# Cross-attention block with MLP on one core: two stages with fp32r operands, against one pipeline over the batches with operands as two fp16 parts

## The reference, cut to what matters

```python
# B=16 batches, L=256 queries, T=256 tokens, D=512, H=16 heads of 32, MLP width 2048, all fp32
q = ln(x, q_norm_g, q_norm_b);  kv = ln(ctx, kv_norm_g, kv_norm_b)
qp = q @ Wq.T + bq;  kp = kv @ Wk.T + bk;  vp = kv @ Wv.T + bv
scores = qh @ kh.T / sqrt(32)                       # per batch and head, 256 x 256
scores += -spatial_scale[h] * dist(query_xy, token_xy) + spatial_offset[h]
scores = where(mask, scores, -inf)
attn = softmax(scores) @ vh                         # per head
x = x + attn @ out_proj_w.T + out_proj_b
h = ln(x, mlp_norm_g, mlp_norm_b)
x = x + gelu(h @ w1.T + b1) @ w2.T + b2             # w1: 2048 x 512, w2: 512 x 2048
```

## Time and profile before

| | us |
|---|---|
| median of 3 runs | 1420.79 (1420.65 to 1423.2) |
| the profiled execution | 1420.8, its span 1419.0, mean clock 0.992 |
| busy: PE, DVE, ACT, POOL | 1381.1, 859.4, 811.9, 706.7 |
| DMA | 120.01 MB, mean 85 GB/s |

### The profile page before, as it was taken

The page is one execution under the profiler, slowest core; times in us unless marked ns, Lnnn a source line. Parts: engine busy times, 40 slices in busy tenths (PEclk is TensorE's granted clock), DMA queues, the critical chain, the costliest instruction groups (busy, mean ns, idle before and its releaser), DMA issues.

```text
span 1419.0 us, 25885 instructions
## 1 busy us (share of the span) xinstructions
PE 1381.1 (97%) x8860; PEld 1166.1 (82%) x8860; DVE 859.4 (61%) x2557; ACT 811.9 (57%) x2003; POOL 706.7 (50%) x1049
## 2 busy tenths in 40 slices
PE   6899999999999999999899999999999999999999
PEld 2589888898888889888688888888888888888887
DVE  6599999999999999989835322232222322223211
ACT  4599989898989999998734323222222222222221
POOL 2588888889888888899621201212012120121200
PEclk9899999999999999999999999999999999999999
DMA  4545555565555556455421100101001010010000
GB/s 172 135 101 126 137 147 144 141 156 134 147 131 130 141 138 157 126 145 147 160 104 38 60 1 0 60 1 60 1 1 60 1 60 1 0 60 0 31 1 30
DMA packets 67076, 120.01 MB, mean 85 GB/s; under 512 B 9088, under 2 KB 9344, under 8 KB 66944
## 3 DMA queue, kind: packets, MB, share of 16 engines
q1 hardware_dynamic: 66944, 118.35, 30.3%
HBM read 50.94 MB, written 16.78 MB: 48 GB/s over the span
## 4 chain that ended last, share of the span: by engine, by line
PE 62%; DVE 16%; POOL 7%; issue 6%; ACT 5%; DMA 2%; SPq 1%; DVEq 0%; ACTq 0%; POOLq 0%
PE ps_s L571 12%; PE ps_qk L557 12%; PE ps_pt L571 12%; PE ps_tr L557 12%; DVE pT L839 4%; PE ps_qk L490 4%; DVE soft L829 3%; POOL soft L1121 3%; POOL soft L1129 2%; PE ps_pt L453 2%; PE ps_vo L516 2%; PE ps_vo L513 2%; DVE qk_parts L845 1%; ACT soft L657 1%; DVE stats L877 1%
## 5 line engine op out<-in xcount | busy, mean ns | idle before, releaser
L978 DVE TENSOR_TENSOR hid<-gelu,hid 128x512 fp32r<-128x512 f32 x128 | 94.7, 740 | 509.7 <-ACT hid L747 509.7
L1121 POOL TENSOR_SCALAR soft<-soft,row_stats 128x256 f32<-128x256 f32 x512 | 246.6, 495 | 58.8 <-DVE row_stats L835 58.2
L657 ACT ACTIVATE soft<-soft,row_stats 128x256 f32<-128x256 f32 x512 | 255.5, 507 | 0.3
L490 PE MATMUL ps_qk<-xT,w_qkv_sb 128*128 128x256 f32 x1536 | 230.8, 293 | 3.3 <-DVE qk_parts L845 3.2
L490 PEld LDWEIGHTS ps_qk<-xT,w_qkv_sb 128*128 128x128 f32 x1536 | 196.9, 192 | 4.3 <-DVE qk_parts L845 4.1
L571 PE MATMUL ps_s<-w,hid 128*128 128x512 f32 x768 | 199.2, 395 | 0.0
L1129 POOL TENSOR_SCALAR soft<-dist,scale_neg,offset 128x512 f32<-128x512 f32 x256 | 197.1, 770 | 0.2 <-ACT dist L681 0.2
L571 PE MATMUL ps_pt<-w,hid 128*128 128x512 f32 x768 | 195.3, 390 | 0.0
L829 DVE CUSTOM_DVE_ANT_0 soft<-ps_s,soft 128x256 f32<-128x256 f32 x512 | 193.0, 413 | 3.8 <-POOL soft L1129 2.0
L557 PE MATMUL ps_qk<-hT,w 128*128 128x512 f32 x768 | 184.8, 389 | 0.9 <-ACT gelu L744 0.9
L557 PE MATMUL ps_tr<-hT,w 128*128 128x512 f32 x768 | 184.6, 389 | 0.0
(11 more groups left out here) (97 smaller groups left out, 2012.7 us busy)
## 6 DMA issues: line engine op xcount, KB each, us to landing
stack<-qk_parts SPq DMA_DIRECT2D x256, 192.0 KB
raw<-in_ctx SPq DMA_DIRECT2D x32, 256.0 KB, 3.2
raw<-in_x SPq DMA_DIRECT2D x32, 256.0 KB, 3.1
x_t<-in_x SPq DMA_DIRECT2D x32, 256.0 KB, 2.6
x_scratch<-x_t SPq DMA_DIRECT2D x32, 256.0 KB, 2.7
x_g<-x_scratch SPq DMA_DIRECT2D x32, 256.0 KB, 3.4
w_raw<-in_w SPq DMA_DIRECT2D x8, 1024.0 KB, 8.0
out<-x_g SPq DMA_DIRECT2D x32, 256.0 KB, 2.2
```

What stands on the lines that cost most here:

```text
L490: mm = e.matmul(ps_qk[:, which * L:(which + 1) * L], w_qkv_sb[:, wp, k, col:col + P], xT[:, b % 2, which, xp, k, :], start=(k, wp, xp) == ...
L657: e.activation(soft[:, ring, lc, :], soft[:, ring, lc, :], ACT.Exp, scale=-1.0, bias=neg_max[:, ring, lc:lc + 1], accum_out=row_sum[:, rin ...
L978: e.tensor_tensor(hid[s % 3][:, LO, :], gelu[:, s % 2, :], hid[s % 3][:, HI, :].bitcast(F32), ALU.subtract).then_inc(s_hlo)
L1121: e.tensor_scalar(soft[:, ring, lc, :], soft[:, ring, lc, :], row_inv[:, ring, lc:lc + 1], P_SCALE, ALU.mult, ALU.mult).then_inc(s_norm)
```

## The change

- One table of slots for everything, slots -26 to 302. Attention of a batch runs in 16 slots; its MLP follows 31 slots behind (`UP`), one step of 128 hidden units per slot, and the down step 11 slots later (`DOWN`). So from slot 31 to 256 a slot holds one head's attention, one up step and one down step. The residual stays in SBUF (`x1`, a ring of 6 tiles); the scratch for x goes.
- MLP up works on the 256 tokens of a batch, 12 matmuls of 256 columns a step into one bank (`ps_up`), which `up_out` on ACT copies out. Gelu and the split of the hidden part work on chunks of four steps (1024 elements per partition): `mlp_gelu`, `hid_hi`, `hid_lo`, two chunks every eighth slot.
- All operands are pairs of fp16. Weights and activations are scaled by factors from norms (the root of sums of squares of gains, shifts and weights) that are made on the chip at the start: `columns_square`, `weight_square`, `chunk_square`, `totals_qkv`, `totals_rest`, `norms_*`, `gains_*`. Each chunk of W_1 and W_2 (1 MB) is loaded twice: once to be squared, once to be split.
- W_2 is split once, stored in HBM (`store_w2`) and streamed, 256 KB per down step, through a ring of 3 (`load_w2`).
- P is split by POOL (`normalise`, HI) and DVE (`p_lo`) in its natural layout, and turned by a transposing DMA, one of 256 KB per head (`p_turn`); the turns of P on PE and `p_hi` on ACT go.
- The layer norm of the MLP has its gain in the weights and its shift in a bias row, four more fp32 rows (`w1_row`); `g_affine` goes. Rings are shorter: soft 5, dist 2, stack 2. Banks: one `ps_up`, two `ps_down`; `ps_vo` also takes the turned x and h. `dist_sqrt` runs per batch.

```diff
-        SOFT_RING, PT_RING, STACK_RING, DIST_RING = 7, 6, 3, 4
+        SOFT_RING, NAT_RING, PT_RING, STACK_RING, DIST_RING, X1_RING, U_RING, HID_RING, W2_RING = 5, 3, 6, 2, 2, 6, 3, 2, 3
+        UP = 31
+        DOWN = UP + 11
+        FIRST_SLOT, LAST_SLOT = -26, DOWN + N_STEPS + 4
...
+            def p_turn(i):
+                gate.wait_ge(s_plo, 2 * i + 2)
+                if i >= PT_RING:
+                    gate.wait_ge(s_pv, (i - PT_RING) // 4 + 1)
+                src = p_nat[:, i % NAT_RING, :, :, :].rearrange("p w c t -> p (w c t)")
+                e.dma_start_transpose(pT[:, i % PT_RING, :, :], src).then_inc(s_pt[i % PT_RING], DMA)
...
+            def load_w2(s):
+                if s < MT:
+                    gate.wait_ge(s_w2st[s // CH], CH * DMA)
+                gate.wait_ge(s_m2, s - W2_RING + 1)
+                e.dma_start(w_2_sb[:, s % W2_RING, :, :].bitcast(F32).rearrange("p w n -> p (w n)"), w2_dram[s % MT]).then_inc(s_w2[s % W2_RING], DMA)
...
+            def load_chunk(tensor, c, second):
+                n = n_chunk(tensor, c)
+                if not second:
+                    gate.wait_ge(s_wsq, 4 + n - 1)
...
+            def mlp_up(s):
+                b, m = divmod(s, MT)
+                gate.wait_ge(s_hlo, n_half(b, 1))
+                gate.wait_ge(s_wlo, 4 + N_CHUNKS)
+                gate.wait_ge(s_u, s)
+                gate.wait_ge(s_brow_sb, 3)
+                for k in range(KT):
+                    for wp, xp in PASSES:
+                        mm = e.matmul(ps_up[:, 0:L], w_1_sb[:, wp, k, m * P:(m + 1) * P], hT[:, b % 2, xp, k, :],
+                                      start=(k, wp, xp) == (0, 0, 0), stop=(k, wp, xp) == (KT - 1,) + PASSES[-1])
+                mm.then_inc(s_m1)
...
+            def mlp_down(s):
+                b, m = divmod(s, MT)
+                chunk, i = divmod(s, CH)
+                gate.wait_ge(s_hidlo, chunk + 1)
+                gate.wait_ge(s_w2[s % W2_RING], DMA * (s // W2_RING + 1))
...
             for slot in range(FIRST_SLOT, LAST_SLOT + 1):
...
+                for i in due(slot, -1, ITEM, N_ITEMS):
+                    scores(i)
...
+                for s in due(slot, UP, ITEM, N_STEPS):
+                    mlp_up(s)
+                for which in range(2):
+                    for G in due(slot, QK_PROJ + which, GROUP, N_HG):
+                        for _ in range(STEPS):
+                            next(qk)
...
+                for G in due(slot, 7, GROUP, N_HG):
+                    attend(G)
+                for s in due(slot, DOWN, ITEM, N_STEPS):
+                    mlp_down(s)
...
+            def chunk_square(n):
+                gate.wait_ge(s_wc[n % 2], DMA * (n // 2 + 1))
+                gate.wait_ge(s_wsq, 4 + n)
+                e.activation(square_out[:], c_stage[n % 2][:].rearrange("p k n -> p (k n)"), ACT.Square, accum_out=ssq[:, n:n + 1]).then_inc(s_wsq)
...
+            def up_out(s):
+                chunk, i = divmod(s, CH)
+                gate.wait_ge(s_m1, s + 1)
+                gate.wait_ge(s_hidlo, chunk - U_RING + 1)
...
+                e.activation(u[:, chunk % U_RING, i, :], ps_up[:, 0:L], ACT.Identity, scale=factor[:, 6:7],
+                             bias=bias_1[:, s % MT:s % MT + 1]).then_inc(s_u)
...
+                for i in due(slot, 0, ITEM, N_ITEMS):
+                    exps(i)
...
+                for s in due(slot, UP, ITEM, N_STEPS):
+                    up_out(s)
+                for half_b in due(slot, UP + 9, 8, 2 * B):
+                    mlp_gelu(2 * half_b)
+                    mlp_gelu(2 * half_b + 1)
+                    hid_hi(2 * half_b)
+                for half_b in due(slot, UP + 11, 8, 2 * B):
+                    hid_hi(2 * half_b + 1)
+                for b in due(slot, -8, BATCH, B):
+                    dist_sqrt(b)
...
             def inverse(i):
+                part = row_inv[:, i % SOFT_RING, :]
                 gate.wait_ge(s_exp, 2 * i + 2)
+                gate.wait_ge(s_plo, 2 * (i - SOFT_RING) + 2)
+                e.reciprocal(part, row_sum[:, i % SOFT_RING, :]).then_inc(s_inv)
+                gate.wait_ge(s_inv, 2 * i + 1)
+                e.tensor_scalar(part, part, P_SCALE, None, ALU.mult).then_inc(s_inv)
...
+            def p_lo(i):
+                ring, nat = i % SOFT_RING, i % NAT_RING
+                for lc in range(LC):
+                    gate.wait_ge(s_norm, 2 * i + lc + 1)
+                    e.scalar_tensor_tensor(out=p_nat[:, nat, LO, lc, :], in0=soft[:, ring, lc, :], scalar=row_inv[:, ring, lc:lc + 1],
+                                           in1=p_nat[:, nat, HI, lc, :], op0=ALU.mult, op1=ALU.subtract).then_inc(s_plo)
```

More of the change, by code:

```diff
@@ L249, in raw_weight, with xT_parts @@
[L249 to L257 removed]
+        def xT_parts(b, n):
+            tok = (n % 2) * P
+            return [xT[:, b % 2, n // 2, part, :, tok:tok + P] for part in (HI, LO)]
@@ L436, in tensor_program, with weight_row @@
+            for ring in range(X1_RING):
+                last = (N_TILES - 1 - ring) // X1_RING
+                e.wait_ge(s_store[ring], DMA * (last + 1))
         def tensor_program(engine):
             e, gate = engine, Gate(engine)
+            def weight_row(sec):
+                gate.wait_ge(s_w[sec], DMA)
+                gate.wait_ge(s_cols, DMA)
+                b_ln = B_Q if sec == SEC_Q else B_KV
+                for k in range(KT):
+                    mm = e.matmul(ps_row[sec][0:1, :], cols_sb[:, b_ln + k:b_ln + k + 1],
+                                  w_stage[sec][:, k, :].rearrange("p (m q) -> p q m", m=KT), start=(k == 0), stop=(k == KT - 1))
+                mm.then_inc(s_brow)
@@ new lines, in w1_row, with totals_qkv @@
+            def w1_row(c):
+                gate.wait_ge(s_wc[c % 2], DMA * (4 + c // 2 + 1))
+                gate.wait_ge(s_brow_sb, 3 + c - 1)
+                for k in range(KT):
+                    mm = e.matmul(ps_down[c % 2][0:1, :], cols_sb[:, B_M + k:B_M + k + 1],
+                                  c_stage[c % 2][:, k, :].rearrange("p (m q) -> p q m", m=KT), start=(k == 0), stop=(k == KT - 1))
+                mm.then_inc(s_brow)
+            def totals_qkv():
+                gate.wait_ge(s_wsum, 3)
+                gate.wait_ge(s_colsum, 1)
+                gate.wait_ge(s_wsq, 3)
+                gate.wait_ge(s_id, ID_ONES)
+                e.matmul(ps_tot[:, 0:19], ones[:], sums[:, 0:19], start=True, stop=True).then_inc(s_tot)
@@ new lines, in totals_rest, with x_turn @@
+            def totals_rest():
+                gate.wait_ge(s_wsum, 5)
+                gate.wait_ge(s_wsq, 4)
+                e.matmul(ps_tot[:, 19:23], ones[:], sums[:, 19:23], start=True, stop=True).then_inc(s_tot)
+            def x_turn(b, n):
+                gate.wait_ge(s_ap, n_tile(b, n))
+                gate.wait_ge(s_id, ID_IDENT)
+                gate.wait_ge(*vo_empty(("x", b, n)))
+                for k in range(KT):
+                    tr = e.transpose(ps_vo[:, k * P:(k + 1) * P], raw[:, n, k * P:(k + 1) * P], ident[:])
+                tr.then_inc(s_xtr)
@@ L630, in qk_hi, with columns_square @@
-            def qk_hi(G):
-                gate.wait_ge(s_qk, 2 * G + 2)
-                if G:
-                    gate.wait_ge(s_stack[(G - 1) % STACK_RING], n_stack(G - 1))
-                gate.wait_ge(s_bcol, N_BCOL[SEC_Q])
-                for which in range(2):
-                    src, hi, _ = qk_of(which)
-                    twice = src.rearrange("p (o l) -> p o l", o=1).to_broadcast([P, 2, L])
-                    e.activation(hi, twice, ACT.Identity, bias=qk_bias(G, which)).then_inc(s_qkhi)
+            def columns_square():
+                gate.wait_ge(s_cols, DMA)
+                e.activation(cols_sq[:], cols_sb[:], ACT.Square).then_inc(s_colsq)
@@ new lines, in v_lo, with qk_lo @@
+            def v_lo(b, tt):
+                hi, lo = [v_parts[:, b % 2, tt, part, :] for part in (HI, LO)]
+                gate.wait_ge(s_vhi, n_half(b, tt))
+                e.tensor_tensor(lo, ps_vo[:], hi, ALU.subtract).then_inc(s_vlo)
+            def qk_lo(G, which):
+                gate.wait_ge(s_qkhi, n_qk(G, which))
+                src, hi, lo = qk_of(which)
+                e.scalar_tensor_tensor(out=lo, in0=src, scalar=qk_bias(G, which), in1=hi[:, 0, :], op0=ALU.add, op1=ALU.subtract).then_inc(s_qklo)
@@ L1097, in gpsimd_program, with norm_powers @@
         def gpsimd_program(engine):
             e, gate = engine, Gate(engine)
+            def norm_powers(first, count, n):
+                gate.wait_ge(s_n2, 5 if n == 0 else 11)
+                gate.wait_ge(s_id, ID_HALF)
+                part = slice(first, first + count)
+                e.tensor_tensor(norm[:, part], norm2[:, part], half[:, 0, 0:count], ALU.pow).then_inc(s_pow)
+                e.tensor_tensor(inv[:, part], norm2[:, part], half[:, 1, 0:count], ALU.pow).then_inc(s_pow)
```

1544 lines of the change are left out of this document (696 added, 848 removed).

## The result

The changed kernel takes 1518.86 us (median of 4 runs, 1518.49 to 1520.5), the kernel before on the same chip 1420.72. The ratio is 1.0691, 95% interval 1.0672 to 1.0709. The forecast was 1390 us, with a range of 1275 to 1510: the time lies outside it, and the kernel got slower where it was to get faster. The profiled execution took 1520.5 us, its span is 1518.7.

A forecast was written before the change was run, and what follows sets the result against it. It took PE to bound the kernel, tied with DVE in attention and alone in the MLP. Slot 31 at 198, remaining PE work 1102, stalls 75 and tail 13 gave 1388, forecast as 1390 us, range 1275 to 1510.

The forecast's parts named there:

- PE's pace: Matmuls with fp16 operands: 0.115 us per 256 columns and 0.220 per 512, PE's sum 1179 us.
- rival D: PE runs at its column rate (sum 1122 us) and ACT's lumps are mostly covered: 1278 us, chance 0.15.
- rival C: fp16 buys no pace on PE, 256 columns at 0.133 and 512 at 0.227: 1498 us, chance 0.12.
- high paces: Upper bounds for fp16 matmuls on PE, 0.133 us per 256 columns and 0.232 per 512: sum given as 1291 us.
- The start: Weight norms and preparation before the first MLP up: slot -5 at 52 us, slot 3 at 87, slot 31 at 198.
- The lump: Gelus, a copy and table loads on ACT every eighth slot, 5.7 to 7.6 us; PE stands 2 us, 32 times: 64.
- The edges of a batch: PE waits for h turned just before its first up, and first down for the last output: some 10 us.
- DVE full, which I exclude by a quarter: In the mixed stage DVE needs 3.35 us per slot against PE's 4.6, so it has slack of a quarter.
- The turn of P: P's transposing DMA priced as a plain copy: 0.43 us to issue on SP, 0.8 us of the engines, hidden.
- Rival B: P's turn by DMA takes the path, from 3.1 us each: 1567 us (1465 to 1670), chance 0.20.
- The end: Behind attention, 42 MLP-only slots of 2.6 us; rival B's sum puts 110 us there.
- 0.03 for something else, slower: The chance left for an outcome outside the forecast and its rivals, something else that is slower.

The follow-up runs named there:

- e4: Changed kernel without the first pass over W_1 and W_2 (eight loads and eight squares on ACT; norms wrong): 1496.9 us.
- e3: Changed kernel without the second pass over W_2; scratch filled once with parts of the key weights, so streamed bytes stay: 1490.9 us.
- e9: Changed kernel with e6 and e8 together, the hidden high part moved from ACT to GpSimd, and W_2's stores one slot earlier: 1499.6 us.
- e6: Changed kernel with the square root of the distances moved from behind two gelus to a slot between two lumps: 1499.8 us.
- e17: Changed kernel with e6, e8 and e15 together and W_2's stores one slot earlier; the hidden copy stays in ACT's lump: 1488.6 us.
- e15: Changed kernel with P_SCALE set to 1, so DVE's small multiply behind the reciprocal goes: 1499.8 us.
- e12: Changed kernel with Exp for Gelu and without the first pass over W_1 and W_2 or the second over W_2; output differs: 1416.6 us.
- e14: Changed kernel with gelus cut to 8 of 256 columns and computing Exp, and the distance root a copy; output differs: 1422.6 us.
- e16: e9 with the hidden high part kept on ACT, behind the exponentials one slot after the gelus, plus e15's edit: 1530.1 us.
- e5: Changed kernel with every turn of P issued a second time into a spare tile that nobody reads: 1542.1 us.
- e8: Changed kernel with the gelus and all behind them (hidden parts, down) one slot later: 1505.7 us.

## Why the prediction was wrong

Its own sum was 198 + 1102 + 75 + 13. By the same terms the trace reads 265 + 1066 + 175 + 13 = 1519: the start is 67 us longer, PE's work 36 shorter, the stalls 100 longer. 1066 is the PE sum at the measured paces, 0.109 and 0.217 for the forecast's 0.115 and 0.220: 1141 in all, less some 75 done by slot 31. 175 is what is left of the 1253.9 us behind the first up once 1066 and the 13 of the tail are taken off.

1. **PE's pace: right in direction, too careful in size.** It is nearly rival D's pace, and rival C is false. The weight loads of 128x128 went from 192 ns in fp32r (L490) to 100 in fp16 (mean of the ups). By the Trainium skill (TensorE: Matmul & The Clock Gate, Weight-path perf modes) such weights, when not FP32, load about twice as fast, and by its gap formula (Back-to-back issue gap) I estimate 109 ns per matmul of 256 columns; this trace agrees with both (100 for 192 ns, 0.109 us). The forecast's sum at the high paces is 1299 by its own bounds; its 1291 takes 0.227 in place of 0.232 for the down steps.
2. **The start: failed, +67 us.** "Slot 31 stands at 198 us." Two parts of this term can be told apart.
   - Up to slot 3, +17: its scores start at 103.6 us, not at 87. The first square starts at 60.4, where the sum has slot -5 at 52, and the eight take 41 us for the sum's 35. The waits for the chunks were in the sum ("35 us for eight slots that would take 20", so 15 us for the pass); without the pass the kernel is 22 us faster (e4).
   - From slot 3 to slot 31, +50: 161 us for 111. The sum had the preparation of W_2 as low parts on DVE. It put ACT's side at nothing: each high part waits, in ACT's order, until the store before it has landed, and PE stands behind. Without the second pass the first up comes 29 us earlier (e3); the earlier store alone gives 10 to 12 (e9 against e6, e17 against e15). The other 20 us stay in e12 (130 us from slot 3 to 31) and are open. The clock of 0.75 in that stage was not in the sum either.
3. **The lump: right mechanism, too small: 98 us for 64.** e14 takes 98 us off the time from first to last up in the profiled runs (96 off the median). I had priced one hand-over (up_out, 2 us, 32 times). Direct waits for up_out are only 32 us between 300 and 1350; more comes through DVE, which stands at the low part of Q for up to 7.00 us, and 35 of the 98 us are PE's longer time for the same matmuls, at a clock of 0.97 instead of 1.00. The text named this path ("DVE, which meets the same lump at hid_lo, passes it on") and left it in the upper bound, 150; in the trace it acts at qk_lo, ahead of hid_lo.
4. **The edges of a batch and what else is left: failed, 77 us for 10.** 77 is what is left of 175 after e14's 98. The forecast named the two waits ("h turned just before its first up; the first down of a batch waiting for the last output") and mis-sized them: in e14's trace PE waits 24.0 us for hT and 15.9 for the residual, 40 us. How the other 37 divide no run here tells.
5. **"DVE full, which I exclude by a quarter": half wrong.** DVE's busy share is 0.74 in the stage, as forecast near 75%. But 980 of 1050 us are its work and its wait in one place of its order, and what is put into this order or taken out reaches PE in part: e15 takes out the small multiply and gains 19 us, and e16, where DVE waits 78 us more for the hidden copy, takes 42 us more than e17.
6. **The turn of P: right that it costs little, wrong as a plain copy.** It takes 1.24 us of SP, not 0.43, 1.5 us of the DMA engines (e5), not 0.8, and 3.2 us to landing. Rival B is false: twice the turns cost 23 us, and the trace shows no idle time of PE before attend. The Trainium skill (DMA: Bandwidth & Descriptors, Latency and other measured facts) gives a turning DMA 261 GB/s, by which I estimate 1.0 us of transfer. In e5 the second turns move 51 GB/s more in 0.30 more of the engines' time, 170 GB/s when the engines are busy, and the measurement decides.
7. **The end: nearly right.** 119 us behind the last scores, where rival B's sum has 110.

No rival named the outcome, unless it is the 0.03 for something else, slower. The time is near C's 1498 by chance only. It would have taken start and stalls above their upper bounds at once: the start came to 265 us for at most 230, the stalls to 175 for at most 150.

## What to carry to other kernels

Before two stages are put side by side, write down for each in-order engine its work and the waits that stand in the middle of it: here 774 and 206 of 1050 us on DVE, and PE's saved time was not collected. Do not add up the gains of small repairs (from first to last up, e6, e8 and e15 give 16 to 20 us each and 20 together). Issue a store a slot before its buffer is wanted when the waiting engine also feeds PE (10 to 12 us here), and do not place a copy late in the slot in which an in-order engine wants it early (e16 against e17, 42 us). Weight preparation in an attention stage costs more than its instructions: the second pass over W_2 is 8.0 us on ACT and 9.4 on DVE, and cost 29.
